# Layer 1 of a four-layer attention and expert kernel: routing in two halves, norms on ScalarE, key work inside the layer before

## The reference, cut to what matters

```python
# layer 1 attention: "decoder" = ctx (64 keys per batch), "encoder" = layernorm(x)
Sim = (enc @ w1)[:, :, None] + (dec @ w2)[:, None, :] + einsum('bid,bjd->bij', enc * w3, dec) + b_sim
A = softmax(Sim, axis=2);  hq_hat = einsum('bij,bjd->bid', A, dec)
Batt = softmax(max(Sim, axis=2), axis=1)
hc_bar = einsum('bi,bid->bd', Batt, enc)          # one row per batch
x += concat([enc, hq_hat, enc * hq_hat, enc * hc_bar], -1) @ W_qv + b_qv
# layer 1 feed-forward, on n = layernorm(x)
scores = sigmoid(n @ gate_w.T)                    # 64 experts in 8 groups of 8
# keep 4 groups by the sum of their two best, then 8 experts, weights normed to 2.5
x += sum_e rw[:, e] * mlp_e(n) + mlp_shared(n)    # shared: 176 hidden columns
```

## Time and profile before

| what | value |
|---|---|
| median of 3 runs | 987.25 us (986.33 to 987.37) |
| the profiled execution | 984.96 us |
| its span in the trace | 983.2 us |
| PE busy in the span | 913.7 us (93%) |
| DVE, POOL, ACT busy | 719.9, 572.7, 521.5 us |

### The profile page before, as it was taken

The page is one execution under the profiler, slowest core; times in us unless marked ns, Lnnn a source line. Parts: engine busy times, 40 slices in busy tenths (PEclk is TensorE's granted clock), DMA queues, the critical chain, the costliest instruction groups (busy, mean ns, idle before and its releaser), DMA issues. The chain is left out here.

```text
span 983.2 us, 16388 instructions
## 1 busy us (share of the span) xinstructions
PE 913.7 (93%) x4925; PEld 700.8 (71%) x4925; DVE 719.9 (73%) x1657; ACT 521.5 (53%) x991; POOL 572.7 (58%) x542
## 2 busy tenths in 40 slices
PE   7897998989896899999999999999999889999796
PEld 5555775666694856888888888888887766667564
DVE  6897776899464788766666666666667888886865
ACT  3455665544634256666666666666663334453354
POOL 5512544677513156777777777777776538884500
PEclk9999999999997989999999999999999689999998
DMA  6000000322000000000000000000002000000001
GB/s 193 1 2 2 1 1 11 88 71 66 12 1 27 2 9 14 25 25 24 24 24 24 24 24 24 24 24 24 25 3 108 1 0 1 1 1 1 1 11 33
DMA packets 27113, 24.01 MB, mean 24 GB/s; under 512 B 3420, under 2 KB 23988, under 8 KB 26804
## 3 DMA queue, kind: packets, MB, share of 16 engines
q1 hardware_dynamic: 27059, 23.34, 8.0%
HBM read 22.28 MB, written 1.05 MB: 24 GB/s over the span
## 5 line engine op out<-in xcount | busy, mean ns | idle before, releaser
L1763 PE MATMUL psum<-xw 128*128 128x512 f32 x1248 | 324.3, 396 | 3.9 <-DVE xw L1400 2.6
L664 POOL TENSOR_TENSOR hh<-arena,hh 128x512 fp32r<-128x512 f32 x176 | 228.2, 1296 | 81.7 <-ACT hh L813 80.0
L1763 PEld LDWEIGHTS psum<-xw 128*128 128x128 f32 x1248 | 233.4, 189 | 56.5 <-issue 7.2
L1599 DVE TENSOR_TENSOR psum<-psum,arena 128x512 f32<-128x512 f32 x176 | 123.1, 700 | 99.6 <-PE psum L1763 93.2
L813 ACT ACTIVATE hh<-arena 128x512 fp32r<-128x512 f32 x228 | 143.1, 629 | 47.7 <-DVE arena L1698 45.3
L1046 ACT ACTIVATE arena<-psum 128x512 f32<-128x512 f32 x176 | 105.3, 598 | 119.0 <-PE psum L1763 118.9
L1763 PE MATMUL psum<-hh,wdn 128*128 128x512 f32 x528 | 148.4, 390 | 0.2 <-POOL hh L664 0.2
L1604 DVE TENSOR_TENSOR arena<-psum,arena 128x512 f32<-128x512 f32 x176 | 121.7, 692 | 8.9 <-DVE psum L1599 2.9
L1763 PEld LDWEIGHTS psum<-hh,wdn 128*128 128x128 f32 x528 | 98.9, 188 | 21.1 <-POOL hh L664 0.5
L1763 PE MATMUL psum<-arena 128*32 128x128 f32 (+7 forms) x1032 | 94.0, 307 | 12.8 <-ACT arena L813 6.5
L612 POOL TENSOR_TENSOR rstd<-veps,neghalf 128x4 f32<-128x4 f32 x28 | 28.2, 1010 | 106.1 <-DVE veps L1238 76.0
(11 more groups left out here) (288 smaller groups left out, 1536.1 us busy)
## 6 DMA issues: line engine op xcount, KB each, us to landing
egu<-in_w SPq DMA_DIRECT2D x44, 128.0 KB, 2.0
egu<-in_egu SPq DMA_DIRECT2D x16, 256.0 KB, 2.6
edn<-in_w SPq DMA_DIRECT2D x44, 64.0 KB, 1.8
edn<-in_edn SPq DMA_DIRECT2D x16, 128.0 KB, 2.0
arena<-in_w SPq DMA_DIRECT2D x1, 1536.0 KB, 6.8
X<-in_x SPq DMA_DIRECT2D x4, 256.0 KB, 4.6
arena<-in_conv SPq DMA_DIRECT2D x1, 1024.0 KB, 8.8
out<-X SPq DMA_DIRECT2D x4, 256.0 KB, 2.3
```

Of the source, the lines that this page charges most:

```text
L664: pool.tensor_tensor(hh[:, s % 4, 1, :], h1[:, s % 2, :], hh[:, s % 4, 0, :].bitcast(F32), ALU.subtract).then_inc(hh_lo, 1)
L1599: dve.tensor_tensor(bank(2 + k), bank(2 + k), sil[:, k, :], ALU.mult).then_inc(prod_done, 1)
L1763: return pe.matmul(dst, lhsT=lhsT, rhs=rhs, start=start, stop=stop)
```

## The change

What it does, part by part:

1. Inside the loop that ends layer 0, PE now also transposes the first two groups of normed rows (after tiles 7 and 11), makes the key bias (after 7) and the first two score rows (after 9 and 13); DVE makes `cw` at tile 1 and the weight scales at tile 11. The scores of one pair of batches come as two products of 64 columns and 256 rows into one bank, in place of one of 128 by 512, and ACT takes each pair in one operation in place of two.
2. PE issues dummy products (`busy`, 9, 9, 3 and 3 of them) between the pieces of the attention.
3. `hc` comes as one column per batch, already transposed: 16 products into `psum[:, 7, 288 + b]`, then one copy. The feature `xcT` is gone: DVE folds hc into the weights (`wfold[:, b] = wqv3 * hc + wqv0`, eight operations of 128x128), and a tile takes three products instead of four, over four PSUM banks instead of three.
4. POOL adds the bias to `X` after the attention's last softmax, not before it.
5. The norm of the feed-forward is applied by ACT (four operations per group, with a bias that POOL makes in two more small operations), not by DVE. PE runs `shared_gate_up` 0 and 1 ahead of the last two groups' transposes.
6. `routing(hf)` runs over 8 tiles, twice. PE transposes the first half's weights ahead of `shared_gate_up(6)`, and spreads them between the four `shared_down` steps; only the second half's are left behind the first two expert steps. POOL copies the first half's weights between its products of the shared expert.
7. ACT loads the table for silu right behind the last sigmoid, ahead of three weight copies.

```diff
@@ tensor: inside the loop that ends layer 0
+                if t == 7:
+                    ln_transpose(2, 0)
+                    ...
+                if t == 9:
+                    sim_rows(0)
+                if t == 11:
+                    ln_transpose(2, 1)
+                if t == 13:
+                    sim_rows(1)
@@ tensor: features
-                for k, feat in enumerate((xnT, hqT, xhT, xcT)):
-                    last = mm(psum[:, 3 + t % 3, 0:D], feat[:, P * t:P * t + P], wqv[:, k, :], k == 0, k == 3)
+            features(0)
+            features(1)
+            for t in range(NT):
+                if t + 2 < NT:
+                    features(t + 2)
+                pe.wait_ge(wfold_done, t // TB + 1)
+                mm(psum[:, QV_BANKS[t % 4], 0:D], xnT[:, P * t:P * t + P], wfold[:, t // TB, :], False, True).then_inc(qv_ready, 1)
+                if t == 9:
+                    ln_transpose(3, 0)
+                if t == 11:
+                    router_logits(0)
+                if t == 14:
+                    ln_transpose(3, 1)
@@ tensor: shared expert and the rows of the weights
+            router_logits(1)
+            pe.wait_ge(x_done, 3 * NT)
+            shared_gate_up(0)
+            pe.wait_ge(xh_lo, E0 + 1)
+            shared_gate_up(1)
+            ln_transpose(3, 2)
+            router_logits(2)
+            ln_transpose(3, 3)
+            router_logits(3)
+            for m in range(2, 2 * NG):
+                if m == 6:
+                    pe.wait_ge(rl_sig, 2)
+                    weights_T(0)
+                    weights_T(1)
+                shared_gate_up(m)
+            ...
+            shared_down(1)
+            weight_rows(0, 0)
+            weight_rows(1, 0)
+            shared_down(2)
+            weight_rows(2, 0)
+            shared_down(3)
+            weight_rows(3, 0)
+            pe.wait_ge(rb_sb[0], 2 * RG)
@@ gpsimd
+                for m in range(2 * NG):
+                    shared_hidden(m)
+                    if m in (3, 4):
+                        weights_twice(m - 3)
@@ scalar
+                act.wait_ge(ln_rstd, NG * 3 + g + 1)
+                for t in range(4 * g, 4 * g + 4):
+                    last = act.activation(xn[:, t, :], X[:, t, :], ACT.Identity, scale=rstd[:, t:t + 1], bias=veps[:, t:t + 1])
+                last.then_inc(ln_xn, 1)
@@ vector
-            routing()
+            routing(0)
+            routing(1)
```

More of the change, by code:

```diff
@@ L204, in build_program @@
         xhT = carve(T)
-        xcT = carve(T)
+        wfold = carve(B, D)
         bt = carve(N)
@@ L449, in build_program @@
         HQ_BANKS = (6, 0, 1, 2)
+        QV_BANKS = (3, 4, 5, 2)
         def hq_part(ap, g):
@@ L987, in _ @@
             act.wait_ge(simT_sb, 1)
[L988 to L997, removed]
+            sim_rows(0)
+            ln_evac_group(2, 1)
+            sim_rows(1)
+            ln_evac_group(2, 2)
+            sim_rows(2)
+            ln_evac_group(2, 3)
+            sim_rows(3)
             for hf in range(2):
@@ L1557, in routing @@
                     at += 2 * k
-                then(dve.tensor_tensor(gs.rearrange("p t g -> p (t g)"), hi[:, :, at], lo[:, :, at], ALU.add))
-                for t in range(NT):
+                then(dve.tensor_tensor(gs[:, r, :].rearrange("p t g -> p (t g)"), hi[:, :, at], lo[:, :, at], ALU.add))
+                if hf == 0:
+                    norm_low(3, 2)
+                for t in ts:
                     last = dve.max(topg[:, t, :], gs[:, t, :])
                 then(last)
-                then(dve.memset(topg[:, :, 4:8], 3.0e38))
@@ L2031, in _, with sim_rows @@
             outputs_T(E0 // 2 - 1)
+            def sim_rows(q):
+                pe.wait_ge(ln_xnT, 2 * NG + q + 1)
+                pe.wait_ge(simT_sb, max(q, 1))
+                if q == 0:
+                    pe.wait_ge(cw_done, 1)
+                if q == 1:
+                    pe.wait_ge(wq_done, 1)
+                for r in range(2):
+                    last = mm(psum[C * r:C * r + C, q % 2, 0:N], cw[:, P * q + C * r:P * q + C * r + C],
+                              xnT[:, 512 * q + N * r:512 * q + N * r + N])
+                last.then_inc(simT_mm, 1)
             pe.wait_ge(pool_made, 1)
@@ L2101, in _ @@
             pe.wait_ge(ctx_in, 16)
-            for b in range(B // 2):
+            for b in range(B):
                 attended(b)
@@ L2106, in _ @@
             for t in range(NT):
[L2107 removed]
+                b, a = t // TB, t % TB
+                last = mm(psum[:, 7, 288 + b:289 + b], xn[:, t, :], btT[:, B * a + b:B * a + b + 1], a == 0, a == TB - 1)
             last.then_inc(hc_mm, 1)
[L2109 to L2113 removed]
```

336 lines of the change are left out of this document (182 added, 154 removed).

## The result

| | median | runs | range | ratio to before, 95% interval |
|---|---|---|---|---|
| before | 985.84 us | 15 | 983.11 to 987.54 | |
| changed | 987.70 us | 15 | 985.48 to 988.98 | 1.0019 (1.0011 to 1.0027) |

The account below looks back on a forecast made before the run. PE, busy 93%, bounds the kernel through the third expert step's start: 356.6 (POOL's second copy) + 25.3 (PE work and waits) + 2.7 (clock fall) = 384.6 against 382.37, so +2.2 us, 989.5 us; range 984.5 to 993.0.

Parts of the forecast that it names:

- The end of layer 0: Extra PE work, 3.9 us, moves the combine's end from 293.6 to 297.5; DVE's last group's norm is ready at 302.0.
- First addition: After the attention, the first addition to X comes at 318.9 instead of 325.50.
- the 10.3 us from which I took the attention's saving: Old stretch to the attention's second maximum, taken as all at half clock; one group left, so 305.1, 3.9 sooner.
- Last addition: End of the features: DVE needs 3.1 us per four tiles, so the last addition ends at 331.6.
- the 8.5 us that I had won up to here: Lead through the end of the features: last addition at 331.6, where before the last statistics stood at 340.2.
- To the shared step 2: Norms by ACT, groups 2 and 3 in series: last logits end 341.3, shared step 2 at 344.2, PE standing 3 us.
- POOL's second copy: Copy of the second quarter of the weights, awaited by PE's step 6, ends at 356.6 through turns with DVE.
- The fall of the clock behind 357: PE stands 2.4 of the 2.9 us before 356.6, so one clock fall is added, 2.7 us.
- To the third expert step: PE's work and waits from 356.6 sum to 25.3 us; with the clock fall the third expert step starts at 384.6.
- Rival 1: DVE and POOL's shared-port lock costs nothing; third expert step at 379.4, -3.0 us, 984.2 us; chance 0.2.
- Rival 2: Clock also falls before 340, delaying logits and copies; with a second fall 3 us in all, 992.5 us; chance 0.13.
- each fall of the clock comes behind a stand of PE: Before the third expert step, falls to 0.50 for 5.4 to 6.4 us follow idle PE, costing about 2.7 to 3.2.

Follow-up runs that it names:

- bias early: Changed kernel with POOL's bias row added to X ahead of the attention's softmax and the block selector made behind it; 988.32 us, one run.
- Other order: Changed kernel with groups 2 and 3 normed, transposed and their logits taken before the two shared steps instead of after; 990.01 us, ratio 1.0047.
- small products: Changed kernel with POOL's eight shared-expert products cut to 8 of their 512 columns; 983.85 us, one run.
- routing whole: Changed kernel with routing over all 16 tiles at once, weight transposes and rows back between second and third expert step; 982.31 us, ratio 0.9964.
- the other order with the copies by ACT: Changed kernel with groups 2 and 3 finished before the two shared steps, and ACT instead of POOL copying the routing weights; 992.51 us, ratio 1.0067.

## Why the prediction came out right

The direction and the size are right, 2.2 against 1.9 us, but the size is luck: it is a sum of terms that missed in opposite directions.

- **The end of layer 0**: 298.6, predicted 297.5. The last group's norm came at 304.0, predicted 302.0: DVE's apply took 1.89 us beside the first of POOL's two selects (302.62 to 303.83), and it was 4.57 instead of 5.35 from combine to transposes once they were away. I had counted turns only for DVE operations on two tensors, and here an operation on one tensor lost one, as did the copy of 4.00 us in "bias early". The Trainium skill, "SBUF — State Buffer", section "SBUF: two separate sides", also names a DVE operation in a 2-port performance mode as one that takes the lock; by that rule this collision could have been forecast. The 1.89 and the 4.00 agree with it, but no row names the mode.
- **First addition**: 321.7, predicted 318.9. Besides the 2.0 above it is the clock: DVE had its folds ready at 320.5 and stood 1.26 us for PE, whose twelve feature matmuls took 2.06 us to the next start, largely at 0.50, where three times four of them at 1.00 take 1.32 (323.55 to 323.99), and the fold product another 0.2. The bias row did stretch DVE's four products, to 4.75 instead of 2.50, and they ended 0.9 behind hc, which I had taken as their cover, but with the first fold done at 320.2 and PE's product of it at 321.00 that cost nothing here. And the 10.3 us from which I took the attention's saving were not all at the half clock, as I wrote: the clock was back at 1.00 from 304.1 on. **Last addition**: 335.4, predicted 331.6. Of the 8.5 us that I had won up to here, 4.7 were.
- **To the shared step 2**: 349.8, predicted 344.2. ACT's four norms took 1.65 instead of 1.28, and group 3's norm stood behind two copies and PE's transposes of group 2 behind two shared steps. The lead should show in the last sigmoid, behind the last logits, after and before:

```profile
346.72 0.60 ACT L1049 ACTIVATE arena<-psum 128x512 f32<-128x512 f32 x1 [1.57 <-PE psum L1816]
```

```profile
347.42 0.60 ACT L1028 ACTIVATE arena<-psum 128x512 f32<-128x512 f32 x1 [1.22 <-PE psum L1763]
```

Of 4.7 us of lead, 0.7 was left here. "Other order" shows that it was mostly the order (its last logits start at 340.54), and "small products" that 1.0 of it was the clock, between the last addition and the shared step 2 (13.4 us there, 14.4 here).
- **POOL's second copy**: ends at 360.2, predicted 356.6, since POOL began at 351.05 and not at 345.7. Its own stretch, 9.2 us, was shorter than my 10.9. The mechanism is right; the turns stretched DVE (6.9 us) more than POOL.
- **The fall of the clock behind 357**, 2.7 us, is the term that failed outright: PE stood 0.92 us for POOL, not 2.4, because it was itself 5 us late. Where it was on time ("other order") the wait of 3.3 us, the fall and the loss were all there.
- **To the third expert step**: 24.6 us, predicted 25.3. From the first down step the prediction's sum is 25.3 - 0.5 - 3.4 = 21.4 (it set the whole 25.3 beside the 19.1 of before, which starts at the down steps); measured are 20.7, and 19.2 with the routing whole, so the new stops cost 1.5 and not 2.3.

So the late start (+3.6 at the second copy) took the place of the fall that did not come (-2.7), with -0.7 in what follows: 384.9 against 384.6. Rival 1 (the lock costs nothing) is refuted by DVE's rows. Rival 2's early fall did come (0.50 from 343.7), and it cost 1.0 to 1.6 us by two kernels with the same code in which it came later, not the 3 of that rival; under the shared steps it cost nothing, since POOL decides there. That each fall of the clock comes behind a stand of PE, as the prediction had it, is refuted by the fall at 319.8. What the prediction said of the whole, that what is won up to the features is given back behind them, holds with numbers: attention part -3.0 us, norm by ACT nothing, halves +5.4. Not tried: the earlier table load by itself, the keys inside layer 0's end by themselves, and the halves with fewer stops on PE, which would tell the 2.9 us apart.

## What to carry to other kernels

Splitting a chain in two to start its first half early pays only if DVE's chain was waited for; here it was ready 0.8 us before PE asked. What it costs is paid in two places: 2.9 of the 4.0 us up to the third expert step are more work and stops in PE's own queue, and 1.1 is the wait for POOL, since the second half was pushed into the stretch in which POOL works without a gap, where a small operation can cost one of POOL's. Before moving DVE work on SBUF tensors, look at what POOL does at the new place. A lead won early must be followed through every in-order queue behind it, ACT's and POOL's too; and dummy products for the clock are worth their place only where PE is the next thing that ends and they do not run past their data.

## What the runs showed of the hardware

- A DVE operation can lose more than one turn: 128x64, alone 0.26 to 0.28 us, took 2.45 across the end of one of POOL's products and its first addition to X (1.26 us) in the other order with the copies by ACT; 128x256, alone 0.42, took 2.72 beside POOL's products of 1.44 us in a row.
- A DVE copy of 128x8 on one tensor, alone 0.17, took 4.00 beside POOL's bias row of 4.52 us, and ended with it.
- The granted clock fell to 0.50 while PE was busy without a gap (4.00 of 4.00 us, in the stretch behind hc); it did so at this place in the profile of every kernel here but that of before, and wider products did not stop it.
- ACT's Identity with a scale and a bias per row took 0.41 us for 128x128, where I had taken 0.32 from a like row.
